# A wait on GpSimd between its scatters, and the tokenizer of the coming pair moved behind the first position output

## The reference, cut to what matters

```
h = concat([class token, patches @ W.T + b] + pos, txt)         # the tokenizer
x = layernorm(h)
key, query phases = tanh(x @ Wk + bk) * pi, tanh(x @ Wq + bq) * pi
V = x @ Wv + bv
retrieved     = causal sum over earlier rows, weighed by cos(query - key phase) @ V
retrieved_pos = the same with phases of the position alone      # the position output
gate  = sigmoid(x @ Wg + bg)
total = gate * retrieved + (1 - gate) * sigmoid(pos_weight) * retrieved_pos
h = h + x + total / norm @ Wo + bo                              # the project product
y = layernorm(h)
shared = (silu(y @ sw1) * (y @ sw3)) @ sw2                      # the shared expert
scores = sigmoid(y @ gate_w.T); top 2 of 64 experts, at most 256 rows of an expert
routed = sum over the two of weight * expert(y)
out = h + shared + routed
```

## Time and profile before

| what | value |
|---|---|
| median of 3 runs | 1853.2 us |
| lowest and highest run | 1828.45, 1863.95 us |
| span of the profiled execution, first to last instruction | 1823.6 us |
| TensorE busy | 1534.0 us (84%) |
| VectorE busy | 1421.6 us (78%) |
| ScalarE busy | 1256.5 us (69%) |
| GpSimd busy | 1226.0 us (67%) |
| scatters of the loop (L605), 768 | 874.1 us busy, mean 1138 ns |
| mean granted clock of TensorE | 0.956 |

### The profile page before, as it was taken

One profiled execution on the slowest core, in us unless ns is written; L12 is line 12 of the kernel. 1 busy time (PEld: TensorE's weight loads), 2 busy tenths in 40 slices (PEclk: granted clock), 3 DMA queues, 4 the chain that ended last, 5 costly groups with the idle time before them and its releaser, 6 DMA issues.

```text
span 1823.6 us, 30829 instructions
## 1 busy us (share of the span) xinstructions
PE 1534.0 (84%) x9237; PEld 1158.6 (64%) x9237; DVE 1421.6 (78%) x5705; ACT 1256.5 (69%) x2195; POOL 1226.0 (67%) x973
## 2 busy tenths in 40 slices
PE   2888998999899999888989898999889975676672
PEld 1566776777676767656767666677667764554552
DVE  3477997999797988777888888889888975587661
ACT  2897997988788878777878787889878851111110
POOL 1025776777676767666667676777667767488887
PEclk9899999999999999999999999999999998899886
DMA  9965666666666666556555655566656221476653
GB/s 182 229 138 120 138 139 125 123 121 124 102 117 100 117 101 106 96 103 103 95 101 104 108 102 102 101 111 105 103 103 103 63 59 40 96 116 109 98 88 35
DMA packets 267117, 197.21 MB, mean 108 GB/s; under 512 B 65464, under 2 KB 246437, under 8 KB 266953
## 3 DMA queue, kind: packets, MB, share of 16 engines
q1 hardware_dynamic: 210120, 174.84, 50.2%
q0 software_dynamic: 51200, 17.87, 8.4%
q10 hardware_dynamic: 5633, 2.56, 0.7%
HBM read 86.24 MB, written 85.39 MB: 94 GB/s over the span
## 4 chain that ended last, share of the span: by engine, by line
PE 40%; ACT 22%; issue 11%; POOL 9%; another core or an unknown queue 8%; DVE 7%; DMA 3%; SPq 0%; ACTq 0%; POOLq 0%; DVEq 0%
POOL out_rows L639 6%; PE bank L919 5%; PE bank L999 5%; ACT img L656 5%; ACT xh L739 4%; PE bank L1087 3%; PE bank L982 3%; POOL slot_rows L605 3%; PE bank L946 2%; PE bank L1018 2%; PE bank L1078 2%; ACT xs L726 2%; ACT kq L793 2%; ACT kq L792 2%
## 5 line engine op out<-in xcount | busy, mean ns | idle before, releaser
L605 POOL DMA_INDIRECT slot_rows<-xs,slot x768 | 874.1, 1138 | 284.5 <-issue 247.3
L656 ACT ACTIVATE img<-img 84x980 f32<-84x980 f32 x190 | 339.6, 1788 | 14.8 <-DMA img<-in_x 7.2
L591 POOL TENSOR_TENSOR rs<-ve,neg_half 128x12 f32<-128x12 f32 (+1 forms) x66 | 150.3, 2277 | 234.4 <-DVE ve L1342 232.8
L919 PE MATMUL bank<-img,w_tok 126*128 126x392 f32 (+1 forms) x640 | 228.7, 505 | 27.9 <-DMA img<-img 23.3
L639 POOL DMA_INDIRECT out_rows<-img,etok x128 | 198.7, 1552 | 64.0 <-issue 35.0
L919 PEld LDWEIGHTS bank<-img,w_tok 126*128 126x128 f32 (+1 forms) x640 | 124.0, 195 | 113.3 <-issue 23.3
L982 PEld LDWEIGHTS bank<-pos_a,v 128*128 128x128 f32 x768 | 145.4, 198 | 54.0 <-issue 10.8
L982 PE MATMUL bank<-pos_a,v 128*128 128x325 f32 (+2 forms) x768 | 163.8, 351 | 6.1 <-issue 3.8
L726 ACT ACTIVATE xs<-h,nb,rs 128x128 f32<-128x128 f32 x384 | 154.0, 481 | 3.0 <-DVE nb L1348 3.0
L739 ACT ACTIVATE xh<-h,nb,rs 128x128 f32<-128x128 f32 x384 | 154.0, 480 | 1.3 <-DVE nb L1348 1.3
L1499 DVE TENSOR_TENSOR h<-bank,hbo 128x768 f32<-128x768 f32 x64 | 61.1, 955 | 114.6 <-remote 103.3
(11 more groups left out here) (217 smaller groups left out, 3697.1 us busy)
## 6 DMA issues: line engine op xcount, KB each, us to landing
img<-in_x SPq DMA_DIRECT2D x384, 150.1 KB
img<-img SPq DMA_DIRECT2D x254, 160.8 KB
img<-img SPq DMA_DIRECT2D x128, 128.6 KB
out_rows<-fin SPq DMA_DIRECT2D x128, 128.0 KB
slot_rows<-xs,slot POOLq DMA_INDIRECT x768
slot_rows<-init_rows SPq DMA_DIRECT2D x16, 540.0 KB, 9.1
img<-slot_rows SPq DMA_DIRECT2D x32, 270.0 KB
h<-in_txt SPq DMA_DIRECT2D x64, 128.0 KB
```

Source lines behind the costliest of these rows:

```text
L591: g.tensor_tensor(out=rs[:, q.u, half:], in0=ve[:, q.u, half:], in1=neg_half[:, half:], op=ALU.pow).then_inc(S["p_rs"], 1)
L605: g.indirect_dma_start(out=slots_d, out_offset=bass.IndirectOffsetOnAxis(ap=slot[0:nt, q.x, r, part:part + 1], axis=0), in_=xs[0:nt, q.x, ...
L656: a.activation(cols[:, b0:b0 + nb, :], raw[:, q.u, :].rearrange("p (t b) -> p b t", b=P)[:, b0:b0 + nb, :], ACT.Copy)\
L919: ins = mm(bank[:, 5, 0:2 * PATCHES], w_tok[r, m, :], xk[r, k.u, :, m, :], start=(m == 0), stop=(m == SHIFT - 1))
```

## The change

**On GpSimd**, ahead of the last part of each pair's scatter (part 5) it now waits for `pe_wo` to reach the count of pair k-5.

**On TensorE**, `token` moves from behind the shared products to behind `position_out_1`, ahead of all shared products. It writes to bank 3 in place of 5 and waits for `a_th` in place of `a_g`. The shared products change order (1a, 1b, then the first position output, 3a, 3b) and banks (3a to 4, 3b to 5). The shared output no longer waits for the token sum but for the shared product of its own (`v_su`).

**On VectorE**, the weighed position goes from ahead of the one-hot masks to behind the bias, the text statistics, the either mask, the token sum, the block pairs and the score; the token sum goes ahead of block pairs, and the shared product behind the weighed position.

```
@@ gpsimd body
                 p4 = k.back(4)
+                p5 = k.back(5)
...
                 if p8.runs():
                     scatter(p8, 3)
                     scatter(p8, 4)
+                if p5.runs():
+                    pool.wait_ge(S["pe_wo"], p5.count())
+                if p8.runs():
                     scatter(p8, 5)
@@ token
-                wait(pe, S["a_g"], k, 2)
+                wait(pe, S["a_th"], k, 2)
...
-                    ins = mm(bank[:, 5, 0:2 * PATCHES], w_tok[r, m, :], xk[r, k.u, :, m, :],
+                    ins = mm(bank[:, 3, 0:2 * PATCHES], w_tok[r, m, :], xk[r, k.u, :, m, :],
@@ shared_out
-                wait(pe, S["v_ht"], w, -4)
...
+                pe.wait_ge(S["v_su"], products(w))
@@ counts
                 pe.wait_ge(S["v_bp"], w.count())
+                if not w.back(-2).runs():
+                    pe.wait_ge(S["a_sl"], w.count())
@@ shared products
             def shared_1a(z):
+                wait(pe, S["v_h2"], z, -1)
+                if not z.back(-1).runs():
+                    wait(pe, S["v_fin"], z, 1)
+                if not later(z):
+                    mm(bank[:, 0, 0:L], sw1[:, :], x2_t[:, 0, :], start=True, stop=True)
...
             def shared_3a(z):
                 if not later(z):
+                    wait(pe, S["v_fin"], z, 1)
+                    wait(pe, S["a_g"], z, -2)
+                    mm(bank[:, 4, 0:L], sw3[:, :], x2_t[:, 0, :], start=True, stop=True)
@@ tensor body
                     position_out_1(p2)
+                if k.runs():
+                    token(k)
+                    if first(k):
+                        position_products()
                 if p4.runs():
+                    shared_1a(p4)
                     shared_1b(p4)
                 if p2.runs():
                     position_out_0(p2)
                 if p4.runs():
                     shared_3a(p4)
                     shared_3b(p4)
-                    shared_1a(p4)
-                if k.runs():
-                    token(k)
-                    if first(k):
-                        position_products()
@@ token_sum
-                TT(h_t[:, :, 1:NIMG], bank[:, 5, 0:2 * PATCHES]...
+                TT(h_t[:, :, 1:NIMG], bank[:, 3, 0:2 * PATCHES]...
@@ shared_product
-                    TT(su[:, :, :], sl[:, :, :], bank[:, 3:5, 0:L], ALU.mult)
+                    TT(su[:, :, :], sl[:, :, :], bank[:, 4:6, 0:L], ALU.mult).then_inc(S["v_su"], 1)
@@ vector body
                     indices(p4)
-                if p2.runs():
-                    weigh_position(p2)
                 if p4.runs():
                     one_hot(p4)
...
                 if p4.runs():
                     either(p4)
-                    shared_product(p4)
+                if k.runs():
+                    token_sum(k)
+                if p4.runs():
                     block_pairs(p4)
                     score(p4)
-                if k.runs():
-                    token_sum(k)
+                if p2.runs():
+                    weigh_position(p2)
+                if p4.runs():
+                    shared_product(p4)
```

More of the change, by code:

```diff
@@ L143, in first, with products @@
     return pair.c == 0
+def products(pair):
+    return pair.count() - sum(c <= pair.c for c in LATER)
 def steps(body, begin, end):
@@ L396, in program @@
              v_max v_lohi v_imax v_idx v_hot v_both v_bp v_cnt v_pick v_place v_over v_slot v_fin
-              v_sg  v_sinv
+              v_sg  v_sinv v_su
             a_d0 a_d1 a_d2 a_h a_xh a_xt a_th a_abs a_sin a_qs a_g a_x2 a_x2t a_lgt a_sl a_lg a_small
@@ L1021, in shared_3b @@
             def shared_3b(z):
-                wait(pe, S["v_fin"], z, 1)
-                wait(pe, S["a_g"], z, -2)
                 if later(z):
-                    tr(bank[:, 4, 0:TILE], ident, ident).then_inc(S["pe_f3b"], 1)
+                    wait(pe, S["v_fin"], z, 1)
+                    wait(pe, S["a_g"], z, -2)
+                    tr(bank[:, 5, 0:TILE], ident, ident).then_inc(S["pe_f3b"], 1)
                 else:
-                    mm(bank[:, 4, 0:L], sw3[:, :], x2_t[:, 1, :], start=True, stop=True).then_inc(S["pe_f3b"], 1)
+                    mm(bank[:, 5, 0:L], sw3[:, :], x2_t[:, 1, :], start=True, stop=True).then_inc(S["pe_f3b"], 1)
             def shared_1a(z):
[L1032 to L1035, removed]
+                wait(pe, S["v_h2"], z, -1)
[3 more added lines that the diff above has]
+                    mm(bank[:, 0, 0:L], sw1[:, :], x2_t[:, 0, :], start=True, stop=True)
             def logits(z):
@@ L1044, in shared_1b @@
             def shared_1b(z):
-                wait(pe, S["v_h2"], z, -1)
-                if not later(z):
-                    mm(bank[:, 1, 0:L], sw1[:, :], x2_t[:, 1, :], start=True, stop=True)
+                if later(z):
+                    tr(bank[:, 0, 0:TILE], ident, ident).then_inc(S["pe_f1a"], 1)
+                else:
+                    mm(bank[:, 1, 0:L], sw1[:, :], x2_t[:, 1, :], start=True, stop=True).then_inc(S["pe_f1a"], 1)
             def shared_3a(z):
                 if not later(z):
-                    mm(bank[:, 3, 0:L], sw3[:, :], x2_t[:, 0, :], start=True, stop=True)
+                    wait(pe, S["v_fin"], z, 1)
+                    wait(pe, S["a_g"], z, -2)
+                    mm(bank[:, 4, 0:L], sw3[:, :], x2_t[:, 0, :], start=True, stop=True)
             def transpose_1(k):
@@ L1352, in token_sum @@
                 dve.wait_ge(S["pe_tok"], k.count())
-                TT(h_t[:, :, 1:NIMG], bank[:, 5, 0:2 * PATCHES].rearrange("p (s t) -> p s t", s=2),
+                TT(h_t[:, :, 1:NIMG], bank[:, 3, 0:2 * PATCHES].rearrange("p (s t) -> p s t", s=2),
                    pos_t[:, 1:NIMG].rearrange("p (o t) -> p o t", o=1).to_broadcast([D, 2, PATCHES]), ALU.add)\
```

## The result

The changed kernel takes 2248.0 us in the median (2246.1 to 2250.3, 4 runs) beside 1857.4 us for the kernel before on the same chip: a ratio of 1.218, with a 95% interval of 1.209 to 1.228. 2221 us was forecast, with a range of 2100 to 2320.

A forecast was written before the change was run, and what follows sets the result against it. TensorE, busy 84%, with late semaphores, was taken to bound the kernel. A closed loop of 28.9 us against 22.59 over 60 steps gives 379, plus 8 for the tail, on 1823.6 of span, plus 10: 2221 us, range 2100 to 2320.

The forecast's parts named there:

- half clock: TensorE from the scores on: after a wait of 6.8 us a stretch runs at half speed, 1.6 us each step.
- a ring: Loop from project product through eight scatters, rstd, bias, weighed position and scores to the next project product: 27.3 us a step.
- named as signs: Expected in the changed profile: GpSimd waits some 9 us on the project product, VectorE and TensorE 6 to 7 us each.
- the fast end: GpSimd's eight scatters: taken at the tail's 10.9 us, since VectorE would be idle, in place of the loop's 11.3.
- The tail: From the last residual sum to the last scatter: 47.7 us becomes 55.2, and the experts wait for it, +8 us.
- The 10 us added to the span: Added to the 2211 us span to get the forecast time, for the spread of run times above the span.
- The clock doesn't stay full: Denies the rival that GpSimd's wait costs the loop but not TensorE's clock: 2124 us, chance 0.2.
- The late semaphore doesn't stay: Denies the rival that SyncE's spreads alone delay the project product's signal, 1.7 us a step: 2324 us, chance 0.1.
- The late semaphore: VectorE's second residual sum starts 3.9 us after the project product it awaits; such pauses sum to 103.3 us over 39 steps.
- The nearly free wait: Rival: without overlap of scatters and spreads signals come on time, each step falls to 20.0 us: 1678 us, chance 0.03.
- The 6.8 us of TensorE's coming wait cover that: The moved tokenizer wants its spreads at most 5.6 us sooner; TensorE's wait ahead of the scores hides this.
- 1.1 us in a tight step: Without GpSimd's wait, the weighed position behind the bias would delay TensorE's scores from 720.15 to about 721.2.

The follow-up runs named there:

- the fill: Changed kernel with 40 useless turns of the identity into a free bank on TensorE ahead of the scores: 2111.7 us, step 27.28 us.

## Why the prediction was right, step by step

Project product to project product in the step shown, 1009.57 to 1038.76:

| term | forecast, us | measured, us |
|---|---|---|
| project product to first scatter | 0.3 | 1010.37 - 1009.57 = 0.80 |
| eight scatters | 10.9 | 1020.76 - 1010.37 = 10.39 |
| rstd and its release | 2.4 | 1023.25 - 1020.76 = 2.49 |
| bias to the end of the weighed position | 2.3 | 1025.54 - 1023.25 = 2.29 |
| release, scores to the end of the project product | 11.45 | 0.10 + 11.22 = 11.3 (with the fill: 1020.24 to 1031.46) |
| half clock | 1.6 | 1038.76 - 1025.64 - 11.22 = 1.9 here; 29.39 - 27.28 = 2.1 in the mean |
| sum | 28.9 | 29.2 here; 29.4 in the mean step |

- **The mechanism** was right: a ring through GpSimd, VectorE and TensorE, closed by one count. The measured step with the clock kept up, 27.28 us, is the forecast's 27.3. That they agree so closely is partly luck: the first scatter was put 0.5 us too early and the eight scatters 0.4 to 0.5 us too slow, and the two cancel.
- **The waits** that were named as signs came: GpSimd 11.1 us a step on the project product (9 forecast; its twelve scatters run faster than in the rows that the forecast was taken from, and the step is longer), VectorE 5.1 us ahead of the bias here and 6.9 on the other chip (6 to 7 forecast), TensorE 6.0 ahead of the scores (6 to 7 forecast).
- **The scatters' speed**: the fast end was chosen, and all eight ran at it, even faster than in the tail. The scatter of 1.71 us before is the first of part 4, which is ahead of the wait and not among the eight; the slow one among those is of part 1 (1.72 us). After, part 4 takes 1.18 and 1.17 and part 1 the same. The reason isn't shown. The Trainium skill's rule on the shared port (SBUF — State Buffer, SBUF: two separate sides), that GpSimd can't write descriptors while VectorE holds it, gives the fast end for an idle VectorE. VectorE wasn't idle here: it was busy for 5.63 of the 10.39 us of the eight scatters, and for 7.15 of the 11.30 us before. No run tests the port by itself.
- **The half clock** was sized by busy time in one stretch (1.6 us). It is 2.1: the stretch at the half clock falls in each step on the scores and what follows. This is the largest error of the sum for a step, 30 us in all.
- **The first scatter** was put at 0.3 us, the gap between two scatters. It comes 0.80 us behind the product's end in each step: GpSimd starts 0.5 us later out of a wait than out of a scatter. Why isn't shown.
- **The tail** was forecast at +8 and is +14.1. The part up to the last scatter, 53.9 against 47.7, is +6.2, where 55.2 had been worked out. The other 7.9 lie behind it, in the experts (274.1 against 266.2 us), and are absent between the two kernels on another chip (257.9 and 257.7). Each is one execution, so they aren't shown to come from the change.
- **The 10 us added to the span** were wrong. In each of the runs that has both, the time is 2 us above the span; the 5 to 30 us in the forecast compared one execution's span with the times of others. The changed kernel's span was forecast at 2211 and is 2248.2: 28 us more in the steps, 6 in the tail, 3 in the start. The 10 us hid a part of that, which is luck, and the forecast of the time is 27 us off.
- **The rivals.** The clock doesn't stay full: the scores run at the half clock in all 59 steps, and the fill shows what that costs. The late semaphore doesn't stay (the last point of this list). The nearly free wait was said to hang on whether the awaited product is done when GpSimd gets there, and with k-6 in place of k-5, where it is, the wait costs nothing.
- **What was said of the tokenizer** holds with the wait and fails without it. "The 6.8 us of TensorE's coming wait cover that" is right: with both parts TensorE waits 0.85 us for the spreads, inside idle time. "1.1 us in a tight step" for the move without the wait is wrong twice: what isn't the spreads costs 0.2 us, and the spreads cost 3.45, which that sentence left out. It was not a term of the sum.
- **With both parts**: the move costs 29.39 - 27.27 = 2.1 us of the step on top of the wait, since it puts the weighed position into the ring. The forecast's 2.28 for that stretch replaces the 1.7 to the counts, and the scores (1.25) come inside too. The two parts don't add: 3.67 + 7.13 would be 10.8 us, and it is 9.25.
- **The late semaphore** was assigned to an overlap of GpSimd's scatters and SyncE's spreads. Its size is shown (22.59 against 20.14 us a step), its cause isn't, but two traces of the chip that has it narrow it down. In the changed kernel the spreads are still issued across the end of the project product, in 49 of 59 steps, while GpSimd is quiet. Here is SyncE's row beside the step shown, where the product ends at 1009.57:

```profile
1004.34 5.82 SPq L463 DMA_DIRECT2D img<-img  x6
```

The residual sum starts 0.04 us behind the product in all 59 steps, where before it came over 0.3 us behind in 54. So SyncE's spreads alone don't make it late, and the rival by which the late semaphore stays is wrong. What is left are 29 waits without a recorded releaser in the loop, 17 of ScalarE and 12 of VectorE. Here are ScalarE's from 154 to 1920 us:

```profile
ACT sl L763 <- PE bank L1061: 79.1, 33, 4.2
ACT sl L763 <- remote: 58.7, 17, 5.9
```

All 29 fall beside a running scatter, and in none of them does SyncE issue anything. The other chip has the first of these rows (80.4 us) and not the second. So an issue of SyncE at the same time isn't needed, and scatters seem to be; but the 29 are at two places of the step only, so that is no proof. What in the scatters would do it, and why on one chip only, stays open: the experiment without scatters met a chip where there was nothing to remove.

No version here that leaves nothing out is faster than the kernel before on the same chip.

## What to carry to other kernels

Before a wait is added, write down what is queued behind it on its engine, follow who waits for the last of that, and see if the path leads back to the event that the wait awaits; if it does, everything on it is now in series, and the sum of its durations is the new step. The price is then set by the count that is awaited and by how much is queued behind (1.4 us for each scatter added here), not by the idle time that the profile shows on the waiting engine. A transfer that arrives just in time is a term too: a consumer that is moved ahead of it waits. And a wait of TensorE can cost more than itself. Behind the waits of some 6 us ahead of the scores the half clock followed in every step, behind those of 2.4 us in the mean ahead of the moved tokenizer in most, and behind those of 0.9 us in the mean ahead of the tokenizer of the changed kernel in 2 of 58.

## What the runs showed that was not expected

- One chip has the late semaphores and three others don't: 22.59 against 20.14 us a step for the same kernel. On the chip that has them, the residual sum was on time in every step of the changed kernel, in which GpSimd is quiet across the end of the project product. A gain or loss measured on one (1.22) isn't the one on another (1.34). The changed kernel, bound by its ring, shows 29.39 on both chips where it ran.
- 40 useless products a step made the kernel 118 us faster, since the half clock behind a wait cost more than they did.
- In the kernel with the tokenizer's move alone the half clock can cost as much as the wait that brings it: a wait of 3.06 us, and then 6.59 us for a tokenizer of 3.46. In the mean it costs half as much (1.3 us a step, beside 2.3 of waits).
